# A decoder layer on one core: the output side of cross attention for two sequences at a time

## The reference

```python
x = x + attn(layernorm(x), W_qkv)
# cross attention, H = 16, D_K = 8:
scores = einsum('bhqd,bhkd->bhqk', q, k) / sqrt(D_K)      # masked, then softmax
o = einsum('bhqk,bhkd->bhqd', softmax(scores), v)          # heads joined: B, S, 128
x = x + o @ Wo.T + bo
x = x + ffn(layernorm(x))                                  # three quantised products
```

## Time and profile before

| | us |
|---|---|
| median of 3 runs (lowest, highest) | 335.33 (334.88, 337.07) |
| the profiled execution: its time | 336.41 |
| its span on the core | 334.6 |
| PE, PEld busy in the span | 302.0, 202.1 |
| DVE, ACT, POOL busy in the span | 277.2, 257.7, 190.5 |

### The profile page before, as it was taken

One profiled execution on the slowest core, in us unless ns is written; L12 is line 12 of the kernel. 1 busy time (PEld: TensorE's weight loads), 2 busy tenths in 40 slices (PEclk: granted clock), 3 DMA queues, 4 the chain that ended last, 5 costly groups with the idle time before them and its releaser, 6 DMA issues.

```text
span 334.6 us, 9852 instructions
## 1 busy us (share of the span) xinstructions
PE 302.0 (90%) x3703; PEld 202.1 (60%) x3703; DVE 277.2 (83%) x651; ACT 257.7 (77%) x465; POOL 190.5 (57%) x339
## 2 busy tenths in 40 slices
PE   2899999999999999999999998999966669578996
PEld 1587877777656666666666665854322224237996
DVE  5358999868889999999999984877789994899753
ACT  3259888878889998989989897787787756983940
POOL 3458899893338697767668578200077771663000
PEclk9999999999999999999999999999999989999999
DMA  6891346662101566500000000000000000000134
GB/s 153 224 315 37 95 122 189 184 200 94 58 13 64 163 179 185 149 2 5 3 5 4 2 5 2 1 0 0 2 0 1 0 1 0 0 2 1 31 96 125
DMA packets 23753, 22.69 MB, mean 68 GB/s; under 512 B 3545, under 2 KB 21402, under 8 KB 23578
## 3 DMA queue, kind: packets, MB, share of 16 engines
q1 hardware_dynamic: 22170, 21.78, 21.6%
q10 hardware_dynamic: 1536, 0.28, 0.5%
HBM read 15.75 MB, written 6.31 MB: 66 GB/s over the span
## 4 chain that ended last, share of the span: by engine, by line
PE 53%; DVE 22%; issue 7%; DMA 6%; POOL 5%; ACT 5%; SPq 1%; POOLq 0%; DVEq 0%; ACTq 0%
DVE mxs L1788 9%; PE banks L695 9%; PE banks L751 9%; PE banks L977 7%; PE banks L1036 6%; DVE nm L1562 3%; DMA X3T<-m_dram 3%; PE banks L625 3%; PE banks L773 3%; PE banks L769 2%; PE banks L618 2%; DVE G L1858 2%; PE banks L764 2%; POOL rstd L369 1%; PE banks L688 1%
## 5 line engine op out<-in xcount | busy, mean ns | idle before, releaser
L1562 DVE TENSOR_REDUCE nm<-banks 128x4 f32<-128x512 f32 x128 | 84.8, 686 | 6.1 <-PE banks L695 2.6
L1235 ACT ACTIVATE PT<-banks,bmask,vmask 128x1024 f32<-128x1024 f32 x64 | 76.8, 1201 | 2.7
L977 PE MATMUL banks<-X3T,upT 128*128 128x512 f32 x96 | 45.9, 622 | 12.3 <-DVE mxs L1788 8.9
L565 POOL TENSOR_TENSOR G<-ng,sq 128x1536 int32<-128x1536 int32 (+3 forms) x10 | 27.9, 2789 | 36.4 <-DVE sq L1819 36.4
L695 PE MATMUL banks<-kd,qd 32*128 32x128 f16 x512 | 47.7, 217 | 0.5 <-DVE nm L1562 0.4
L1788 DVE TENSOR_REDUCE mxs<-G 128x1 f32<-128x1536 int32 (+3 forms) x30 | 42.2, 1424 | 4.3 <-ACT G L1293 3.8
L751 PE MATMUL banks<-PT,VP 128*32 128x128 f32 x1024 | 41.2, 279 | 0.0
L977 PEld LDWEIGHTS banks<-X3T,upT 128*128 128x128 f32 x96 | 18.0, 197 | 38.4 <-issue 18.1
L695 PEld LDWEIGHTS banks<-kd,qd 32*128 32x128 f16 x512 | 27.0, 92 | 20.4 <-issue 11.6
L1077 ACT ACTIVATE h<-X,shift,rstd 128x128 f32<-128x128 f32 x64 | 26.3, 484 | 11.2 <-POOL shift L414 11.1
L751 PEld LDWEIGHTS banks<-PT,VP 128*32 128x32 f32 x1024 | 24.1, 109 | 9.3 <-issue 3.2
(11 more groups left out here) (198 smaller groups left out, 722.9 us busy)
## 6 DMA issues: line engine op xcount, KB each, us to landing
kd<-k_dram SPq DMA_DIRECT2D x32, 128.0 KB, 2.7
qd<-q_dram SPq DMA_DIRECT2D x32, 128.0 KB, 2.7
ctxg<-in_ctx_dram SPq DMA_DIRECT2D x8, 256.0 KB, 3.2
X3T<-m_dram SPq DMA_DIRECT2D x1, 1792.0 KB, 10.8
out_dram<-y SPq DMA_DIRECT2D x7, 256.0 KB, 2.3
X<-in_x_dram SPq DMA_DIRECT2D x3, 512.0 KB, 10.3
k_dram<-khi SPq DMA_DIRECT2D x7, 128.0 KB, 1.8
k_dram<-klo SPq DMA_DIRECT2D x7, 128.0 KB, 1.9
```

Source lines behind the costliest of these rows:

```text
L565: nc.gpsimd.tensor_tensor(GI[:, c], ng[:, u, part], sq[:, u, part], ALU.mult).then_inc(S["b_t"], 1)
L977: m = pe.matmul(bank(2 + FC * (g % 2) + k), w[:, k * P:k * P + P], grp(X3T, g), start=True, stop=True)
L1235: act.activation(PT[:, a, :], bank(2 + 2 * a, 2), ACT.Exp, bias=bmask[:, n:n + 1], scale=vmask[:, n:n + 1]).then_inc(S["t_exp"], 1)
L1562: V.tensor_reduce(nm[:, n % 2, c:c + NSET], bank(u).rearrange("p (h m) -> p h m", m=P), AX.X, ALU.max, negate=True).then_inc(S["t_max"], 1)
```

## The change

Sequences 0 to 27 (`PR` = 28) are taken in 14 pairs, called units; sequences 28 to 31 are units of one. For a pair the two sequences' `pv` outputs share one bank (columns 0 to 511), and each step of the output side is made once for both:

- `out_copy` copies 512 columns and not 256, `turn_copy` and `project_copy` 256 and not 128, `add_rows` adds 256;
- `queries` makes four transposes, `turn` two, `project` two products;
- `attend` takes a reciprocal of 32 values and a multiplication of 256 columns.

The order changes too. For unit `u` (sequences 2u, 2u + 1) `queries` moves into the second half of sequence 2u + 2, where `project` was, and `turn` and `project` stand in their old places, in sequence 2u + 3. ScalarE does, in an even sequence `n`, `probs(n, 0)`, `project_copy(n//2 - 2)`, `out_copy(n//2 - 1)`, `max_copy(n + 1)`, `probs(n, 1)`, and in an odd one `probs(n, 0)`, `max_copy(n + 1)`, `probs(n, 1)`, `turn_copy(n//2 - 1)`. VectorE does `attend` in odd sequences and both `stat3` in even ones; `aggregate3`, `largest3`, `roots3` and `rows3` move by up to one sequence, and `mvar` of the third normalisation gets a second buffer. In the last four sequences the order is as before.

```diff
@@ -51,6 +51,8 @@
 EARLY = NG - 1 - GB
 FC = 3
 TAIL = 3
+PR = 28
+NP = PR // 2
 QB = 32
 EPS = 1e-5
 MAGIC = 12582912.0
...
@@ -149,11 +151,11 @@
         nm = sb("nm", [P, 2, H], where=early)
         NM = sb("NM", [P, P], BF16, where=early)
         mT = sb("mT", [P, 2, P], BF16, where=early)
-        orec = sb("orec", [P, H], where=early)
-        oun = sb("oun", [P, 2 * P], where=early)
-        on_ = sb("on_", [P, P], where=early)
-        wo = sb("wo", [P, 2, P], where=early)
-        oT = sb("oT", [P, P], where=early)
+        orec = sb("orec", [P, 2 * H], where=early)
+        oun = sb("oun", [P, 4 * P], where=early)
+        on_ = sb("on_", [P, 2 * P], where=early)
+        wo = sb("wo", [P, 2 * P], where=early)
+        oT = sb("oT", [P, 2 * P], where=early)
         early.close()
 
         def q_parts(g):
...
@@ -234,6 +236,35 @@
 
         def live(g):
             return 0 <= g < NG
+
+        def unit_of(n):
+
+            return n // 2 if n < PR else n - PR + NP
+
+        def members(u):
+
+            return (2 * u, 2 * u + 1) if u < NP else (u + PR - NP,)
+
+        def span(u):
+
+            k = len(members(u))
+            return slice(members(u)[0] * P, (members(u)[0] + k) * P)
+
+        def pair_bank(u):
+
+            return bank(6 + u % 2)
+
+        def kept(u):
+
+            return slice(0, 2 * P) if u < NP else slice(u % 2 * P, u % 2 * P + P)
+
+        def project_columns(u):
+
+            return slice(2 * P, 4 * P) if u < NP else slice(P, 2 * P)
+
+        def mvar3(g):
+
+            return norms[2]["mvar"][:, g % 2 * 2 * GB:(g % 2 + 1) * 2 * GB]
 
         def wait(eng, name, value):
 
...
@@ -523,8 +554,10 @@
                     maxima_split(n + 2)
                 if n == B - 2:
                     roots3(NG - 2, slice(0, GB))
-                if 1 < n < B - 1:
-                    add_rows(n - 2)
+                if n > PR and n < B - 1:
+                    add_rows(unit_of(n - 2))
+                elif n > 2 and n % 2 == 0 and n <= PR:
+                    add_rows(n // 2 - 2)
                 if n == 1:
                     last_keys_halves()
                 if 1 < n < 4:
...
@@ -533,12 +566,10 @@
                     add_constant(n)
                 if n in (9, 13, 17):
                     weight_values(n // GB - 2)
-                if n > GB and n % GB == 2 and n < B - 2:
+                if n > GB and n % GB == 3 and n < PR:
                     roots3(n // GB - 1, slice(0, GB))
-                if n > GB and n % GB == 3 and n < B - 1:
-                    rows3(n // GB - 1, 0)
-                if n >= 2 * GB and n % GB == 0:
-                    rows3(n // GB - 2, 1)
+                if n >= 2 * GB and n % GB < 2:
+                    rows3(n // GB - 2, n % GB)
             rows3(NG - 2, 0)
             rows3(NG - 2, 1)
 
...
@@ -757,20 +789,26 @@
                 pe.wait_ge(S["t_nm"], n + 1)
                 pe.transpose(bank(2).bitcast(BF16)[:, 0:P], NM[:, :], identb[:, :]).then_inc(S["t_mT"], 1)
 
-            def queries(n):
-
-                pe.wait_ge(S["t_ou"], n + 1)
-                for a in range(2):
-                    m = pe.transpose(bank(6 + n % 2)[:, (2 + a) * P:(3 + a) * P], oun[:, a * P:(a + 1) * P], ident[:, :])
+            def queries(u):
+
+                pe.wait_ge(S["t_ou"], u + 1)
+                for c in range(2 * len(members(u))):
+                    m = pe.transpose(pair_bank(u)[:, c * P:(c + 1) * P], oun[:, c * P:(c + 1) * P], ident[:, :])
                 m.then_inc(S["t_tr"], 1)
 
-            def turn(n):
-                pe.wait_ge(S["t_o"], n + 1)
-                pe.transpose(bank(6 + n % 2)[:, 0:P], on_[:, :], ident[:, :]).then_inc(S["t_oT"], 1)
-
-            def project(n):
-                pe.wait_ge(S["t_oTc"], n + 1)
-                pe.matmul(bank(6 + n % 2)[:, P:2 * P], oT[:, :], WXT[:, 3, :], start=True, stop=True).then_inc(S["t_wo"], 1)
+            def turn(u):
+                pe.wait_ge(S["t_o"], u + 1)
+                for c in range(len(members(u))):
+                    m = pe.transpose(pair_bank(u)[:, c * P:(c + 1) * P], on_[:, c * P:(c + 1) * P], ident[:, :])
+                m.then_inc(S["t_oT"], 1)
+
+            def project(u):
+                pe.wait_ge(S["t_oTc"], u + 1)
+                first_column = project_columns(u).start
+                for c in range(len(members(u))):
+                    m = pe.matmul(pair_bank(u)[:, first_column + c * P:first_column + (c + 1) * P], oT[:, c * P:(c + 1) * P],
+                                  WXT[:, 3, :], start=True, stop=True)
+                m.then_inc(S["t_wo"], 1)
 
             for i in range(NG - 1):
                 if i == 1:
...
@@ -906,43 +944,49 @@
                 pe.wait_ge(S["t_exp"], 2 * n + 1)
                 if n + 1 < B:
                     max_rows(n + 1)
-                if n > 0:
-                    queries(n - 1)
+                if n >= PR:
+                    queries(unit_of(n - 1))
                 pe.wait_ge(S["t_vp"], 2 * n + 2)
-                if n < 2:
-                    pe.wait_ge(S["l_qhi"], NG - 1 + n)
+                if n in (0, 2):
+                    pe.wait_ge(S["l_qhi"], NG - 1 + n // 2)
                 if n == B - 1:
                     pe.wait_ge(S["t_xd"], 1)
-                elif n > 1:
-                    pe.wait_ge(S["t_wc"], n - 1)
+                elif n > 3:
+                    pe.wait_ge(S["t_wc"], unit_of(n) - 1)
                 pv(n, 0)
                 if n + 1 < B:
                     pe.wait_ge(S["t_mTc"], n + 2)
                 first_half_bank(n, 0)
-                if n > 0:
-                    turn(n - 1)
+                if n >= PR:
+                    turn(unit_of(n - 1))
+                elif n > 2 and n % 2:
+                    turn(n // 2 - 1)
                 second_half_bank(n, 0)
                 if n == 0:
                     queries2(NG - 1)
                 pe.wait_ge(S["t_exp"], 2 * n + 2)
                 pv(n, 1)
                 first_half_bank(n, 1)
-                if 0 < n and n != B - 2:
-                    project(n - 1)
+                if n >= PR and n != B - 2:
+                    project(unit_of(n - 1))
+                elif n < PR and n > 2 and n % 2:
+                    project(n // 2 - 1)
+                elif n < PR and n > 1:
+                    queries(n // 2 - 1)
                 second_half_bank(n, 1)
                 if n == B - 2:
-                    project(n - 1)
+                    project(unit_of(n - 1))
 
             for n in range(B):
                 cross(n)
 
-            queries(B - 1)
+            queries(unit_of(B - 1))
             for g in range(3):
                 turn_early_rows3(g)
-            turn(B - 1)
+            turn(unit_of(B - 1))
             pe.wait_ge(S["u_tca"], 1)
             turn_weights3(0, 0)
-            project(B - 1)
+            project(unit_of(B - 1))
             for g in range(3, NG - 2):
                 turn_early_rows3(g)
             pe.wait_ge(S["u_tca"], 2)
...
@@ -1208,21 +1252,22 @@
...
+            def out_copy(u):
+                act.wait_ge(S["t_pv"], 2 * members(u)[-1] + 2)
+                wait(act, "t_tr", u)
+                c = slice(0, 2 * P * len(members(u)))
+                act.activation(oun[:, c], pair_bank(u)[:, c], ACT.Copy).then_inc(S["t_ou"], 1)
+
+            def turn_copy(u):
+                act.wait_ge(S["t_oT"], u + 1)
+                wait(act, "t_wo", u)
+                c = slice(0, P * len(members(u)))
+                act.activation(oT[:, c], pair_bank(u)[:, c], ACT.Copy).then_inc(S["t_oTc"], 1)
+
+            def project_copy(u):
+                act.wait_ge(S["t_wo"], u + 1)
+                wait(act, "t_x2", u if u < NP else max(u - 1, NP))
+                act.activation(wo[:, kept(u)], pair_bank(u)[:, project_columns(u)], ACT.Copy).then_inc(S["t_wc"], 1)
...
@@ -1245,27 +1290,33 @@
             probs(0, 1)
             probs(1, 0)
             queries_copy(NG - 1)
-            out_copy(0)
             max_copy(2)
             probs(1, 1)
-            turn_copy(0)
             for n in range(2, B):
                 probs(n, 0)
-                out_copy(n - 1)
-                if n < B - 1:
-                    project_copy(n - 2)
+                if n >= PR:
+                    out_copy(unit_of(n - 1))
+                    if n < B - 1:
+                        project_copy(unit_of(n - 2) - (n == PR))
+                elif n % 2 == 0:
+                    if n > 2:
+                        project_copy(n // 2 - 2)
+                    out_copy(n // 2 - 1)
                 if n + 1 < B:
                     max_copy(n + 1)
                 probs(n, 1)
-                turn_copy(n - 1)
+                if n >= PR:
+                    turn_copy(unit_of(n - 1))
+                elif n > 2 and n % 2:
+                    turn_copy(n // 2 - 1)
 
             def weights_copy(m_, w, n):
                 act.wait_ge(S["f_t"], m_ + 1)
```

(91 more changed lines are left out.)

## The result

The changed kernel takes 342.52 us (median of 4 runs, 341.65 to 342.84), the kernel before, on the same chip, 336.02 (334.88 to 337.07): a ratio of 1.0204, 95% interval 1.0167 to 1.0241. The profiled execution has 341.65 us, span 339.9 (before 336.41, span 334.6).

A forecast was written before the change was run, and what follows sets the result against it. With three engines nearly full, a loop of dependences through TensorE, VectorE and ScalarE was taken to set the pace: 7.88 us a pair against 7.23. 7.8 - 0.7 + 0.8 = +7.9 gave 335.33 + 7.9 = 343.2 us, range 337.5 to 346.5.

The forecast's parts named there:

- Step 1: TensorE, even sequence's second half: pv 0.58, first bank 0.33 and queries 0.58 until the second bank starts, 1.49 us.
- Step 2: Second bank to turn, through VectorE's reciprocal (+0.10) and multiplication (+0.13): 1.66 grows to 1.89 us.
- Step 3: TensorE from turn (0.38) through second bank, pv and first bank to the start of project: 1.61 us.
- Step 4: project, ScalarE's three copies, probs(n, 1) and the hand-over until TensorE starts pv: 2.89 us.
- The sum: The four legs of the loop of dependences: 7.88 us for a pair against 7.23, 0.65 more.
- the twelve periods: Between the 13 paired turn steps of sequences 3 to 27: 12 x 0.65 = 7.8 us lost.
- the stretch ahead of them: Sequences 1 and 2 lose output-side blocks, half of 1.22 us given back in sequence 3: -0.7 us.
- the one behind them: Sequence 28 does the last pair with all blocks doubled, plus a short wait: +0.8 us.
- TensorE's own work: TensorE's blocks for a pair, without waits, fall from 7.16 to 6.69 us.
- A: Rival, faster: no waits appear and TensorE's 6.69 us sets the pair's pace, giving 329.2 us; chance 0.09.
- the loop of the prediction: Dependences through TensorE, VectorE's attend, and ScalarE's copies and probs, setting a pair's time at 7.88 us.
- Grouping: Joined ScalarE copies save some 0.2 us a pair; one skill rule gives 333, the other, agreeing with the trace, a loss.

The follow-up runs named there:

- half_attend: Changed kernel, but attend takes the reciprocal of 16 values and the product of 128 columns for each pair: 339.69 us, ratio 1.0106.
- both_halves: Changed kernel, but out_copy moves 256 columns and attend does one sequence for each pair: 341.07 us.
- reordered_agg: Changed kernel with queries, attend and turn at sequence heads, project_copy behind max_copy, aggregate3 in sequence 4g + 3: 335.20 us, 0.9996 of the kernel before.
- queries_in_gap: Changed kernel with queries moved between the two banks of the even sequence's first half: 350.12 us, 1.0408 of the kernel before.

## Why the prediction was right

- **Step 1**, from `pv` of the even sequence's second half to its second bank: 157.23 - 155.74 = 1.49, predicted 1.49.
- **Step 2**, to `turn`: 159.13 - 157.23 = 1.90, predicted 1.89. From the reciprocal's start to the multiplication's is 0.38 where it was 0.29, from there to `turn` 0.48 where it was 0.34: the two estimates of +0.10 and +0.13 came out as +0.09 and +0.14. half_attend took 0.23 back.
- **Step 3**, to `project`: 152.80 - 151.19 = 1.61, predicted 1.61.
- **Step 4**, to `pv` again: 155.74 - 152.80 = 2.94, predicted 2.89. The products were over after 0.71; `wo` was taken 0.04 later and held ScalarE 0.28 (predicted 0.02 and 0.26), `oun` 0.48 and `mT` 0.16 (0.48, 0.17), and the exponentials with the hand-over 1.27 (1.25). This is the step that was mis-sized, by 0.05.
- **The sum**, 7.94 against 7.88. Over the stage +8.5 against +7.9: the twelve periods gave +8.4 (+7.8 forecast), the stretch ahead of them -0.8 (-0.7), the one behind them +0.9 (+0.8). Step 4 alone makes 12 x 0.05 = 0.6, the difference between the two.
- **TensorE's own work**: a pair has its waits of 0.43 and 0.46, and the even sequence's first `pv` starts 0.30 behind `max_rows` where the odd one's starts 0.16 behind it (157.56 to 157.72), 0.14 more. If that too is waiting, 7.94 less 1.03 leaves 6.91, where 6.69 was predicted; the windows agree (26.16 / 30 x 7.94 = 6.92). So this term was 0.2 too low. It is in no step of the loop and did not touch the sum, but A's 329.2 would have been too low as well. No kernel ran at this pace, so the figure is read from the waits.
- **What was not seen**: VectorE's leg, as long as the loop of the prediction in every other pair. The prediction called the second reductions early by TensorE's waits; over the sequences 4g + 2 they are not, VectorE has no pause from the first reduction to `attend`. The diff moves `aggregate3`, and the prediction has no term for it. That the forecast held all the same, because this leg was not longer, is luck.
- **The time**: 342.52 against 343.2. The loop's loss was 0.6 larger than forecast and the rest of the span 3.2 smaller; the kernel before came out 0.7 higher when it was run again. That the time agrees to 0.7 us is partly luck; the mechanism does not rest on it.
- **Grouping**: joining the copies did save ScalarE time (busy 257.7 us before, 251.9 after) and saved none in the kernel. The Trainium skill, "Perfetto Trace Analysis", section "Optimizing Scalar/DVE Operations", ties the gain from grouping to a saturated engine, and advises breaking instructions up where engines that aren't saturated cause bubbles on others. For the change as it stands the trace agrees with the second: 7.93 for a pair against 7.23. No run tests it by itself: both_halves leaves work out and does not break it up, and reordered_agg has the grouped operations at 7.22.

## What to carry to other kernels

Where several engines are over 90% busy, follow one item around the loop, from engine to engine, and add up the legs; grouping lengthens each leg it touches by the added columns while it saves only fixed costs, and the saving shows as idle time. Look for the second-longest leg before halving the longest: here they were equal to 0.01 us in every other pair. Look at the order before the widths: the same grouped operations cost 2% in one order and nothing in another.

## What the runs showed of the hardware

- The reciprocal from PSUM takes 247 ns for 16 columns and 346 for 32, about 6 ns for each further column; from SBUF it took 378 for 36. The multiplication from PSUM takes 291 for 128 columns and 424 for 256, 1 ns a column. Groups by form of the changed kernel on VectorE:

```profile
...
L1681 DVE RECIPROCAL orec<-banks 128x32 f32<-128x32 f32 x14 | 4.8, 346 | 0.0
...
L1681 DVE RECIPROCAL orec<-banks 128x16 f32<-128x16 f32 x4 | 1.0, 247 | 1.0 <-PE banks L796 1.0
...
```

- A copy of 512 columns from PSUM shows 0.59 us and holds ScalarE 0.48 (153.83 to 154.31); one of 256 columns shows 0.38 and holds it 0.28 (153.55 to 153.83).
- TensorE's clock can fall in the middle of a stage in which TensorE is nearly full on average: in queries_in_gap it went to 0.50 behind two microseconds with 1.21 busy and a wait of 0.83, and the pair took 2.6 us more. The same two microseconds two pairs earlier (1.21 busy, a wait of 0.83) left it at 1.00, so they are not enough by themselves.
